# A graph network of 14 stages: edges between the same two nodes are summed on the vector engine, scatters write instead of adding, and the five unweighted stages gather 14 node tiles in place of 10

## The reference

```python
agg = segment_sum(h[src], dst, num_segments=N)                # unweighted: 5 such stages
x   = segment_sum(w[:, None] * x[src], dst, num_segments=N)   # weighted: 3 layers x 3 hops = 9 stages
```

## Time and profile before

| | us |
|---|---|
| median of three runs | 9865.39 (9837.11 to 9877.95) |
| profiled execution, its own time | 9867.92 |
| its span, first to last instruction | 9866.1 |
| mean granted TensorE clock | 0.863 of full speed |
| first matmul of stage 0 | 1615.31 after the start |

### The profile page before, as it was taken

The page is one execution under the profiler, slowest core; times in us unless marked ns, Lnnn a source line. Parts: engine busy times, 40 slices in busy tenths (PEclk is TensorE's granted clock), DMA queues, the critical chain, the costliest instruction groups (busy, mean ns, idle before and its releaser), DMA issues.

```text
span 9866.1 us, 149234 instructions
## 1 busy us (share of the span) xinstructions
PE 7979.3 (81%) x61517; PEld 7721.7 (78%) x61518; DVE 2055.5 (21%) x7806; ACT 538.6 (5%) x1640; POOL 5582.5 (57%) x5057
## 2 busy tenths in 40 slices
PE   1999003998989999898878878789787878888788
PEld 1999003998989889897878878788787878878787
DVE  2555100001111100111112222221121322212133
ACT  0000000000000000000000000000000000000000
POOL 0488888647655564764536455453654545555453
PEclk5555557999999999998989989899898989989899
DMA  9972224787878778786656666666566666666665
GB/s 403 354 240 0 0 0 111 259 260 220 260 218 263 226 246 265 224 270 208 215 190 227 205 210 222 198 217 216 194 214 203 221 198 211 214 210 213 217 220 184
DMA packets 720692, 2079.04 MB, mean 211 GB/s; under 512 B 266702, under 2 KB 457458, under 8 KB 551902
## 3 DMA queue, kind: packets, MB, share of 16 engines
q1 hardware_dynamic: 312018, 1639.12, 48.0%
q0 software_dynamic: 296944, 252.44, 12.9%
q10 hardware_dynamic: 111132, 178.79, 4.8%
HBM read 1788.54 MB, written 281.36 MB: 210 GB/s over the span
## 4 chain that ended last, share of the span: by engine, by line
PE 39%; another core or an unknown queue 21%; issue 18%; POOL 14%; DMA 5%; ACT 1%; DVE 1%; ACTq 0%; POOLq 0%; DVEq 0%; SPq 0%
PE pwide L903 30%; POOL counts L521 8%; PE pstep L928 6%; POOL ring_f L545 3%; DMA counts<-zz 3%; POOL weights L521 3%; PE pwide L941 1%; PE pwide L976 1%; DMA counts<-count_val,count_idx 0%; ACT zz L633 0%; DMA ring_f<-table,f_src 0%; DMA weights<-wgt_val,wgt_idx 0%; PE pwide L945 0%; ACT zz L642 0%
## 5 line engine op out<-in xcount | busy, mean ns | idle before, releaser
L545 POOL DMA_INDIRECT ring_f<-table,f_src x3636 | 3472.5, 955 | 3386.3 <-PE pstep L928 1054.7
L903 PE MATMUL pwide<-hcur,room 128*128 128x128 f32 x23618 | 3009.8, 283 | 905.7 <-DMA room<-counts 610.1
L903 PEld LDWEIGHTS pwide<-hcur,room 128*128 128x128 f32 x23618 | 2864.4, 198 | 1000.1 <-issue 982.6
L903 PE MATMUL pwide<-acc,room 128*128 128x128 f32 x22834 | 2935.8, 284 | 360.8 <-issue 350.1
L903 PEld LDWEIGHTS pwide<-acc,room 128*128 128x128 f32 x22834 | 2792.2, 199 | 439.0 <-issue 424.3
L928 PE MATMUL pstep<-ring_f,hot 128*128 128x128 f32 x8268 | 1283.8, 288 | 215.7 <-issue 176.5
L1303 DVE TENSOR_SCALAR hot<-iota,f_dst,f_wgt 128x128 f32<-128x128 f32 x3159 | 884.3, 353 | 2518.3 <-remote 1313.8
L928 PEld LDWEIGHTS pstep<-ring_f,hot 128*128 128x128 f32 x8268 | 1124.8, 202 | 265.6 <-issue 240.8
L521 POOL DMA_INDIRECT counts<-count_val,count_idx x672 | 1049.6, 1562 | 322.8 <-issue 200.5
L521 POOL DMA_INDIRECT weights<-wgt_val,wgt_idx x536 | 861.7, 1608 | 163.5 <-issue 159.2
L1302 DVE TENSOR_SCALAR hot<-iota,f_dst 128x128 f32<-128x128 f32 x975 | 216.1, 299 | 1539.2 <-remote 1059.0
(11 more groups left out here) (222 smaller groups left out, 1926.0 us busy)
## 6 DMA issues: line engine op xcount, KB each, us to landing
room<-weights SPq DMA_DIRECT2D x693, 1024.0 KB
room<-counts SPq DMA_DIRECT2D x495, 1024.0 KB
counts<-zz ACTq DMA_DIRECT2D x70, 1792.0 KB
room<-weights SPq DMA_DIRECT2D x162, 768.0 KB
weights<-zz SPq DMA_DIRECT2D x56, 1792.0 KB
room<-counts SPq DMA_DIRECT2D x100, 768.0 KB
ring_f<-table,f_src POOLq DMA_INDIRECT x3636
room<-weights SPq DMA_DIRECT2D x63, 512.0 KB
```

The source lines that it names most:

```text
L545: pool.indirect_dma_start(out=ring_f[:, slot, :], out_offset=None, in_=rows_from[:, :], in_offset=bass.IndirectOffsetOnAxis(ap=f_src[:, c: ...
L903: ins = pe.matmul(bank[:, j * P:(j + 1) * P], room[:, n % SLOTS, (o * w + j) * P:(o * w + j + 1) * P], x_of(a)[:, first + o, :], start=beg ...
```

## The change

- `scatter` has no `compute_op`: it writes its value over what lies there.
- So that this gives the same matrix, a new function `summed`, called first in `place`, makes each value a sum. With the key `(dst - first dst of the partition) * 6272 + src`, it compares each edge of a partition with those 1 to 40 behind it (`NEAR`) and adds where keys agree. Of two equal edges the one that is written last has the whole sum. `lanes` become longer by 41 columns for this, and are loaded in two pieces each.
- The test for the fast way now asks that no node has over 41 edges and that a partition's nodes span less than 1024.
- `EARLY` is 14 sparse and 35 dense tiles: it has 608 scatters for 672, 63 zeroing DMAs for 70, 252 gathers a stage for 180, 273 sparse PE steps for 195, and 1715 dense blocks for 1911. `LATE` stays.
- `ZQ` is 2 for 4, `WINDOW` 36 for 26. The weights' lanes are loaded later, with the others of `LATE`.

```diff
-ZQ = 4
+ZQ = 2
+NEAR = 40
+WIDE = 1024
-EARLY = Split([4, 4, 2], [4] * 9 + [3], 160)
+EARLY = Split([4, 4, 4, 2], [4] * 8 + [3], 224)
-WINDOW = 26
+WINDOW = 36
...
+                for by, n in ((0, p.lane), (p.lane, NEAR + 1)):
+                    rows_ = flat_pad[p.edge0 + by:p.edge0 + by + p.lane * P].rearrange("(p t) -> p t", p=P)
+                    sp.dma_start(to[:, by:by + n], rows_[:, 0:n]).then_inc(lanes_in, 16)
-            lane_load(lanes[0][0], dst_pad, EARLY, 0)
-            lane_load(lanes[0][1], dst_pad, EARLY, LAPS)
-            lane_load(lanes[0][2], src_pad, EARLY, 0)
-            lane_load(lane_val[1][:, :], wgt_pad, LATE, 0)
+            lane_load(lanes[0], dst_pad, EARLY)
+            lane_load(lanes[2], src_pad, EARLY)
...
-                    in_=lane_val[which][:, at:at + 1], in_offset=None,
-                    compute_op=ALU.add).then_inc(scattered[q], 16)
+                    in_=lane_val[which][:, at:at + 1], in_offset=None).then_inc(scattered[q], 16)
...
+            def summed(which):
...
+                link(V.tensor_scalar(key, dst, dst[:, 0:1], None, ALU.subtract))
+                if which == 0:
+                    link(V.tensor_scalar(mask, dst, float(N), None, ALU.is_lt))
+                    link(V.tensor_tensor(eq, dst[:, 0:p.lane], dst[:, NEAR + 1:], ALU.is_equal))
+                    link(V.tensor_scalar(part, key[:, 0:p.lane], float(WIDE), None, ALU.is_ge))
+                    link(V.tensor_tensor(eq, eq, part, ALU.add))
+                    link(V.tensor_tensor(eq, eq, mask[:, 0:p.lane], ALU.mult))
+                    V.reduce_sum(same[:, :], eq, axis=mybir.AxisListType.X).then_inc(v_same, 1)
+                    dve.wait_ge(v_same, 1)
+                    link(V.memset(val, 1.0))
+                else:
+                    link(V.tensor_copy(val, wide[:, 0:p.lane]))
+                link(V.scalar_tensor_tensor(key, key, float(TILES * P), src, ALU.mult, ALU.add))
...
+                for k in range(1, NEAR + 1):
+                    inner, outer = slice(0, p.lap - k), slice(p.lap - k, p.lap)
+                    link(V.tensor_tensor(eq, key[:, 0:p.lane], key[:, k:k + p.lane], ALU.is_equal))
+                    add3 = eq3
+                    if which == 1:
+                        V.tensor_tensor(part3[:, :, inner], eq3[:, :, inner], w3[:, :, inner], ALU.mult)
+                        link(V.tensor_tensor(part3[:, :, outer], eq3[:, :, outer], far3[:, :, 0:k], ALU.mult))
+                        add3 = part3
+                    link(V.tensor_tensor(v3[:, :, k:p.lap], v3[:, :, k:p.lap], add3[:, :, inner], ALU.add))
+                    link(V.tensor_tensor(v3[:, :, outer], v3[:, :, outer], add3[:, :, outer], ALU.add))
...
-                dve.wait_ge(lanes_in, 96 + 32)
+                dve.wait_ge(lanes_in, 96 + 96)
```

More of the change, by code:

```diff
@@ L127 @@
 RBLOCKS = -(-MOST // RB)
-LAPS = min(EARLY.lap, LATE.lap)
-WINDOW = 26
+STRIDE = EARLY.lane + 56
+assert NEAR < min(EARLY.lap, LATE.lap) and max(EARLY.lane + NEAR + 1, LATE.lane + LATE.lap) <= STRIDE
+WINDOW = 36
 def turning(beat):
@@ L268, in program @@
         wraw = rflat[:, 6272:6784].rearrange("p (w d) -> p w d", w=4)
-        lanes = [[rflat[:, 6784 + i * EARLY.lane:6784 + i * EARLY.lane + p.lane] for i in range(7)] for p in (EARLY, LATE)]
-        below = lanes[0][3][:, 0:3 * P]
+        lanes = [rflat[:, 6784 + i * STRIDE:6784 + (i + 1) * STRIDE] for i in range(8)]
+        below = lanes[3][:, 0:3 * P]
         rows_f = oflat[:, 4480:4480 + 3 * RBLOCKS * P].rearrange("p (w k e) -> p w k e", w=3, k=RBLOCKS)
@@ L407, in _, with lane_load @@
             sp.wait_ge(pad_out, 48)
[L409 removed]
+            def lane_load(to, pad, p):
                 flat_pad = pad.rearrange("c e -> (c e)")
[L411 to L416 removed]
+                for by, n in ((0, p.lane), (p.lane, NEAR + 1)):
[3 more added lines that the diff above has]
+            lane_load(lanes[2], src_pad, EARLY)
             sp.wait_ge(v_x, 1)
@@ L424, in fast @@
                 sp.wait_ge(lanes_ready, 1)
-                lane_load(lanes[1][0], dst_pad, LATE, 0)
-                lane_load(lanes[1][2], src_pad, LATE, 0)
+                lane_load(lanes[0], dst_pad, LATE)
+                lane_load(lanes[2], src_pad, LATE)
+                lane_load(lanes[7], wgt_pad, LATE)
                 wait_zeroed(sp, EARLY, zeroed_counts, ZQ)
@@ L1088, in place @@
             def place(which):
                 p, val = (EARLY, LATE)[which], lane_val[which][:, :]
-                l_dst, l_dst2, l_src, l_f0, l_f1 = lanes[which][0:5]
-                l_si, l_hi, l_di, l_lo = (v.bitcast(I32) for v in (l_dst, l_src, *lanes[which][5:7]))
+                summed(which)
+                l_dst, l_dst2, l_src, l_f0, l_f1, l_i5, l_i6 = (v[:, 0:p.lane] for v in lanes[0:7])
+                l_si, l_hi, l_di, l_lo = (v.bitcast(I32) for v in (l_dst, l_src, l_i5, l_i6))
@@ L1092, in place @@
                 link(V.tensor_scalar(l_f0, l_dst, float(N), None, ALU.is_lt))
[L1093 to L1097, removed]
                 link(V.tensor_scalar(l_f1, l_dst, float(p.ns * P), None, ALU.is_ge))
                 link(V.tensor_tensor(l_f0, l_f0, l_f1, ALU.mult))
[L1100 to L1103, removed]
+                link(V.tensor_tensor(val, val, l_f0, ALU.mult))
```

9 lines of the change are left out of this document (added).

## The result

The changed kernel takes 10820.53 us in the median of four runs (10793.25 to 10854.56), the kernel before beside it 9868.85 (four runs): a ratio of 1.097 [1.093, 1.101]. It is 9.7% slower; 9451 had been forecast. The profiled execution took 10854.56, with a span of 10852.7.

A forecast was written before the change was run, and what follows sets the result against it. Setup was taken as bound by POOL's scatters, then by VectorE's chain, and the stages by PE starved during gathers. From 9867.9 us, 396 for setup and 21 for early stages came off, giving 9451; range 9330 to 9620.

The forecast's parts named there:

- VectorE's rounds: Setup: 40 rounds of 1.86 us in `summed(0)` and 40 of 2.62 us in `summed(1)`.
- The scatter's price: Setup: a plain scatter costs what a gather does, 0.947 us and 0.30 to the next; 608 end at 1075.
- The rival in which the price stays: Setup: plain scatters stay at 1.866 us and end at 1449, total 9688; chance 0.20 for a price above 1.48.
- a plain write no cheaper than the add: Scatters: if the DMA engine's read-modify-write set the pace, the setup would gain 159 us; the trace was held against it.
- Everything behind it (flag, row fetches, walk) moves by as much: Setup, VectorE's chain: the sums add 76.7 us, shifting all behind them; the walk ends near 1084.
- -4 a stage: Stages 0 to 4: middle of -26 (fewer products) and +18 (more gathers), -21 us in all, ends -132 and +90.
- no gather costs PE more: Stages 0 to 4: PE's loss stays at 76 us a stage, so they gain 132 us; total 9340.
- PE starves on gathers: Stages 0 to 4: at 0.8 us lost a gather, stages grow 99 us each, total 9969; chance 0.05.
- Its sign: Early stages: windows would show PE with fewer records per us than in 2226:2346 over more than 150 us.
- The fetch rule: Unrolled stages: program fetching is mostly hidden; were PE's holes hidden elsewhere, five early stages would gain 132 us; windows spoke against.
- Late stages: Stages 5 to 13: the nine keep their work and stay at 595 us each.
- zeros: Setup: 63 zeroing DMAs for 70 end at about 314 us, so the first scatter comes at about 315.

The follow-up runs named there:

- e7: Changed kernel with a 128-column GpSimd write ahead of each scatter into `counts`: 7708.31 us, ratio 0.934, where the kernel before took 8250.56.
- g1: Changed kernel with a 128-column GpSimd write ahead of each scatter into `counts`, weights unsummed and scattered with the add: 10134.56 us, ratio 1.047.
- f1: Changed kernel, unchanged, rerun in another set: 10740.66 us, ratio 1.110, where the kernel before took 9668.63.
- e2: Changed kernel with the add given back to the scatters of both matrices, split kept: 9800.17 us, ratio 1.011.
- e1: Changed kernel with a 512-column GpSimd write ahead of each scatter into `counts`, all scatters still plain: 10160.38 us, ratio 1.048.
- e3: Kernel before with its scatters writing instead of adding, nothing else changed: 10551.54 us, ratio 1.089.
- c0: Kernel before, unchanged, as reference beside other runs: 8249.86 us, ratio 1.000, where the kernel before took 8250.56.
- f3: Changed kernel with an 8-column GpSimd write ahead of each scatter into `counts`: 10644.77 us, ratio 1.102.
- f2: Changed kernel with a 128-column GpSimd write ahead of each scatter into `counts`: 10646.18 us, ratio 1.101, where the kernel before took 9668.63.
- h1: Kernel before with a 256-column GpSimd write ahead of each gather: 9338.82 us, ratio 0.949, where the kernel before took 9854.93.
- e5: Kernel before with a 256-column GpSimd write ahead of each gather: 8794.34 us, ratio 1.066, where the kernel before took 8250.56.

## Why the prediction was wrong, point by point

**VectorE's rounds: right.** 1.85 and 2.52 us for 1.86 and 2.62; in the changed kernel:

```profile
210.79 0.79 DVE L1117 TENSOR_TENSOR room<-room 128x608 f32<-128x608 f32 x1
...
212.64 0.79 DVE L1117 TENSOR_TENSOR room<-room 128x608 f32<-128x608 f32 x1
```

Stage 0 begins 129 us after the walk's end (1859 to 1988), for 135 forecast (1084 to 1219).

**The scatter's price: right** (0.97 and 0.30, 608 of them from 327 on), except that from 1.27 the period went to about 1.40, so the last ended at 1156 and not at 1075. The rival in which the price stays, with 0.20, is out. The Trainium skill, DMA: Bandwidth & Descriptors, Specifications, has the DMA engine do transfers under 512 bytes as read-modify-write. What the prediction drew from it, a plain write no cheaper than the add, did not come to bear: the pace is GpSimd's own instruction, and that fell from 1.56 to 0.97 us.

**"Everything behind it (flag, row fetches, walk) moves by as much": this step failed first.** It moved the walk by 77 us (measured 79) and left its length at 749. The walk took 1522 us, because the scatters beside it had become short. In place of 1219, stage 0 began at 1988: 769 of the 1404 us by which 9451 missed the profiled 10855. I had asked of the scatter's price only when it ends, not what else runs meanwhile and how it fares at a higher rate. In the free set the reasoning came out: e7's walk took 749 us and its stage 0 began at 1192.

**"-4 a stage" for the early stages: this term failed second,** by 618 us in all (+597 for -21). The loss was priced per gather, at 0.42 to 0.48 us, from traces in which the scatters were long. Two things were mis-sized. The short scatters cost the early stages 421 us (g1 to f1) to 446 (e2 to e1), for nothing in the sum: an adding scatter among the gathers had been a pause in which PE caught up. And the split itself, with the adds restored, costs some 245 us (e2) to 301 (g1), 49 to 60 a stage, where -26 to +18 were allowed; with plain scatters it is 19 (e1 to e3). So the two don't add as separate prices. In the free set the same split gains 25 a stage: there the likeliest case's lower end, "no gather costs PE more", is what came.

**The rival that came was "PE starves on gathers".** It named the early stages and the scatters' shortness, at 0.8 us a gather, but not the walk; measured were 696 - 474 = 222 us of loss a stage, 0.88 a gather. It had a chance of 0.05. Its sign came too: 3400 to 3550 us has 657 records, 4.4 per us, for 5.3 in 2226:2346. Against it stood that the late stages, with more gathers, keep to 0.48 a gather. But a late stage has no scatters and is 595 us long, while the new early one has 360 indirect DMAs at 1.25. And the row that spoke for it, 5120:5162 of the earlier trace rows with 35 records for 376, showed it plainly: where gathers follow one another at 1.25 us, PE does a tenth of its work. Nothing there says that this holds for gathers only.

**The fetch rule.** The Trainium skill, Runtime: NRT & Kernel Launch, Instruction fetch mechanics, has it that fetching a long program is mostly hidden. Our forecast leaned on the windows against this. For the unrolled stages e7 settles what packets can show. Its instruction queues moved as much in stages 0 to 4 (last two lines) as those of the changed kernel (first two):

```profile
q8 instruction: 168, 2.75, 0.3%
q14 instruction: 43, 0.35, 0.0%
q8 instruction: 168, 2.75, 0.5%
q14 instruction: 43, 0.35, 0.0%
```

A packet of q8 takes 0.99 us in the median in the one and 1.01 in the other. Yet e7 has no hole without a releaser there, like c0 with the unchanged program, and the changed kernel has over 600. In the free set the trace thus agrees with the page, and in the held-up one it is not the fetch packets that became more or slower. In the walk, from 500 to 1100 us with 13 of its holes, the instruction queue moved 8 packets, too few for one in each hole. Whether a fetch is asked for late, no record shows.

**Late stages, DMA traffic, zeros:** as forecast (+17 us in nine stages; first scatter 327 for 315).

**Open.** Why a set holds up or not. Why f3's walk is faster than the changed kernel's at almost the same mean period. What passes between GpSimd's descriptor writing and the other engines' sequencers. Why the wait is 0.70 us each time.

## What to carry to other kernels

Making a GpSimd DMA cheaper also makes it more frequent: before counting the gain, look in the trace for a stretch where such DMAs follow one another without pause, and read what the other engines do in it. Price an interference from a stretch with the same spacing of what causes it, not by a mean per piece. On a kernel full of indirect DMAs, time the kernel before beside every variant: here its own time moves by 20% between sets, and the same edit (e7, f2) gains 6.6% in one and loses 10% in another.

## What was unexpected in the hardware

- While GpSimd issues indirect DMAs of 0.97 us some 1.3 us apart, VectorE's register instructions take 0.70 us for 0.057, and a loop of VectorE and TensorE runs at a thirteenth of its speed (0.09 for 1.17 steps per us), with DMA engines idle to two thirds. At 1.48 us it is half the speed, at 1.70 whole. Beside adding scatters alone (1.87 us apart) the loop kept its speed in every run. All this is of the held-up sets.
- In the two free sets none of it happens, in e7 at a period of 1.40 either; the unchanged kernel then takes 453 us a late stage for 596.
- Waiting makes it faster: in a held-up set, 0.33 us of useless work ahead of each gather takes 5.1% off the kernel before (h1); in a free set it adds 6.6% (e5).
- The same 128 values of 4 bytes are 32 packets and 0.97 us as a plain scatter, and 144 packets and 1.56 us as an adding one.
